# Order of the routing steps in a turn of the dilated attention: picks one head later, gate steps dealt one to a head, the gates' turn at the ninth head

## The reference, cut to what matters

```python
t = t + _L3_attn_ref(_ln_t(t), ...)        # 16 heads of 8; segments of 256, 512, ... tokens, dilations 1, 2, ...
# of _L3_ffn_ref(_ln_t(t), ...), the routing:
gate_logits = x @ gate_weight.T            # 16 experts
top_vals, top_idx = jax.lax.top_k(gate_logits, 2)
routing_w = jax.nn.softmax(top_vals, axis=-1)
```

## Time and profile before

| | us |
|---|---|
| median of 3 runs | 3617.76 (3611.89 to 3627.61) |
| the profiled execution | 3635.59 |
| its span, first to last instruction | 3633.8 |
| PE busy | 2827.6 (78%) |
| DVE busy | 2208.3 (61%) |
| ACT busy | 1549.9 (43%) |
| POOL busy | 1040.7 (29%) |
| mean granted TensorE clock | 0.884 |

### The profile page before, as it was taken

The page is one execution under the profiler, slowest core; times in us unless marked ns, Lnnn a source line. Parts: engine busy times, 40 slices in busy tenths (PEclk is TensorE's granted clock), DMA queues, the critical chain, the costliest instruction groups (busy, mean ns, idle before and its releaser), DMA issues. The chain is left out here.

```text
span 3633.8 us, 65093 instructions
## 1 busy us (share of the span) xinstructions
PE 2827.6 (78%) x20886; PEld 1553.7 (43%) x20887; DVE 2208.3 (61%) x4232; ACT 1549.9 (43%) x3274; POOL 1040.7 (29%) x1360
## 2 busy tenths in 40 slices
PE   6777849999999999996599119558888888619998
PEld 3334503433343334332598117435555555403336
DVE  5774547777777777772222116547777777526771
ACT  1113516666666666664355003424444444404440
POOL 0002300122222222223233752214565565620000
PEclk8998959999999999999799559868998888859995
DMA  2002442132213232310322113332333223021123
GB/s 76 0 0 102 184 84 39 37 52 45 51 39 53 42 54 39 53 25 11 103 61 60 41 41 111 103 55 54 60 64 63 61 58 62 24 90 50 51 57 117
DMA packets 209243, 215.62 MB, mean 59 GB/s; under 512 B 33456, under 2 KB 185201, under 8 KB 209009
## 3 DMA queue, kind: packets, MB, share of 16 engines
q1 hardware_dynamic: 187008, 178.05, 21.8%
q0 software_dynamic: 14336, 25.72, 2.7%
q10 hardware_dynamic: 7680, 8.93, 0.7%
HBM read 129.26 MB, written 81.90 MB: 58 GB/s over the span
## 5 line engine op out<-in xcount | busy, mean ns | idle before, releaser
L1539 ACT ACTIVATE attn_exps<-attn_sbank 128x392 f32<-128x392 f32 x1600 | 704.6, 503 | 499.3 <-PE attn_sbank L1456 493.6
L1581 DVE TENSOR_REDUCE attn_mx<-attn_rot 128x1 f32<-128x784 f32 x768 | 722.3, 967 | 191.8 <-PE attn_rot L1469 188.0
L1469 PE MATMUL attn_rot<-attn_k,attn_q 96*128 96x392 bf16 x1536 | 401.6, 344 | 97.1 <-DVE attn_mx L1581 64.6
L2223 ACT ACTIVATE dil_exps<-dil_sbank 128x512 f32<-128x512 f32 x512 | 289.2, 597 | 407.3 <-PE dil_sbank L2121 338.1
L1456 PE MATMUL attn_sbank<-attn_q,attn_k 99*128 99x392 bf16 x1536 | 450.1, 333 | 12.3 <-ACT attn_exps L1539 11.1
L1496 PE MATMUL attn_acc<-attn_exps,attn_v 128*32 128x392 f32 x3584 | 348.4, 500 | 0.0
L2274 DVE TENSOR_REDUCE dil_mx<-dil_rot 128x4 f32<-128x1024 f32 x256 | 307.6, 1219 | 55.4 <-PE dil_rot L2131 53.2
L2131 PE MATMUL dil_rot<-dil_k,dil_q 96*128 96x256 bf16 x1024 | 174.2, 299 | 120.3 <-DVE dil_mx L2274 83.2
L1456 PEld LDWEIGHTS attn_sbank<-attn_q,attn_k 99*128 99x128 bf16 x1536 | 148.8, 98 | 270.1 <-ACT attn_exps L1539 133.9
L2661 PE MATMUL silu_ph<-silu_route_w,silu_xT 128*128 x424 | 237.7, 645 | 22.6 <-issue 11.2
L1469 PEld LDWEIGHTS attn_rot<-attn_k,attn_q 96*128 96x128 bf16 x1536 | 117.5, 99 | 303.5 <-DVE attn_mx L1581 201.6
(11 more groups left out here) (370 smaller groups left out, 4863.5 us busy)
## 6 DMA issues: line engine op xcount, KB each, us to landing
attn_q<-q_pieces SPq DMA_DIRECT2D x192, 98.0 KB
attn_k<-k_pieces SPq DMA_DIRECT2D x192, 98.0 KB
silu_x<-silu_rows SPq DMA_DIRECT2D x212, 64.0 KB
dil_q<-dil_q_pieces SPq DMA_DIRECT2D x192, 66.0 KB
dil_k<-dil_k_pieces SPq DMA_DIRECT2D x192, 66.0 KB
q_pieces<-qkv_piece SPq DMA_DIRECT2D x16, 588.0 KB, 3.1
k_pieces<-qkv_piece SPq DMA_DIRECT2D x16, 588.0 KB, 3.2
v_rows<-qkv_v SPq DMA_DIRECT2D x16, 476.0 KB, 3.8
```

Of the source, the lines that this page charges most:

```text
L1469: ins = nc.tensor.matmul(rot[b][:, hf, 0:HS], q[nxt.side][g][0:QROWS, j, c * P:(c + 1) * P], k_[nxt.side][g][0:QROWS, j, cols], start=True ...
L1539: nc.scalar.activation(e_[:, n % NP, :], sbank[(n + t.side) % 3][:, 0:HS], ACT.Exp, scale=A_DIM ** -0.5).then_inc(s_ex, 1)
L1581: nc.vector.tensor_reduce(into, rot[b][:, :, 0:HS], AX.XY, ALU.max).then_inc(s_free, 1)
L2223: nc.scalar.activation(e_[:, k % NP, :], sbank[k % 3][:], ACT.Exp, scale=D_DIM ** -0.5).then_inc(s_ex, 1)
```

## The change

It moves steps in the list and nothing else; no operation is added, dropped or resized.

```diff
             out += [("ranks", lag), ("soft", lag)] + [("place", n, lag) for n in range(5)]
         if h >= 2:
             out.append(("scatter", h - 2, lag))
-        if h == 2:
-            out += [("place", n, lag) for n in range(5, 11)]
-        return out + {4: [("gate", lag)], 5: [("store", lag)]}.get(h, [])
+        if 2 <= h <= 7:
+            out.append(("place", h + 3, lag))
+        if h == 8:
+            out += [("gate", lag), ("store", lag)]
+        return out
...
-                out += [("pick", n) for n in range(16) if 11 + (n + 2) // 4 == h] + [("root",)] * (h == 12)
+                out += [("pick", n) for n in range(16) if 12 + n // 4 == h] + [("root",)] * (h == 12)
```

## The result

The changed kernel takes **3592.60 us** (median of 6 runs, 3585.77 to 3601.91), the kernel before 3615.66 us beside it (6 runs, 3605.21 to 3627.61): a ratio of 0.9933, 95% interval 0.9909 to 0.9957. That is 23 us faster. The forecast was 3575, 43 us faster.

The account below looks back on a forecast made before the run. A full turn was taken as a chain alternating between PE and DVE, neither full. Terms -4.6 + 0.1 + 1.3 + 0.3 = -2.9 us, times 13 -38, last turns -6: -43 from 3617.76 to 3575 us, range 3560 to 3605.

Parts of the forecast that it names:

- Stretch A: From `turn` 1's copy to the sixth head's maximum: gates leaving h=2 to 4 save 4.6 us a turn at full clock.
- B: From the sixth to the tenth head's maximum: +1.3 us for the gates' transposes, +0.1 for small operations.
- h=8: New place of the gates' transposes, ahead of the weighing: +1.3 us a turn, bounds 0.84 and 2.2.
- Picks: Late in the turn, POOL's scaling of the rows holds pick 13 (L937): +0.3 us a turn, bounds -0.3 and +0.3.
- C: From the rows' copy to the next turn's first maximum, where moved picks stand: +0.3 us a turn.
- the 0.5 us that the prediction named as a sign of being wrong: Late in the turn: held picks adding up to more than 0.5 us a turn would refute the forecast.
- SP's queue: `store` at h=8 delays SP's loads 4 to 5 us; about 5 us slack, nothing charged; slower rival 3639 us, chance 0.05.
- which one?: Gain between `turn` 1's copy and the sixth maximum: 4.6 us at the upper clock, 2.9 if the dip stays; took 4.6.
- where the prediction wanted to see 1.00: Sign expected from `turn` 1's copy to the sixth maximum: granted clock 1.00, the 2.4 GHz level.
- the dip stays (or moves along the stretch): Rival, chance 0.22: low clock remains behind 1.29 us of idle PE; gain 2.9 instead of 4.6, -22 in all, 3596 us.
- The tails: Turns 15 and 16: PE's waits ahead of `compact` leave, partly returning ahead of `add`; 0 to -10 us, -6 taken.

Follow-up runs that it names:

- e1_picks_only: The kernel before with only the picks' places moved, gate steps as before: 3621.23 us, ratio 0.9996.
- e4_norm_late: The changed kernel with POOL's scaling of the rows tied to pick 15 instead of pick 9: 3573.31 us, ratio 0.9871.
- e3_fill: The changed kernel with PE's four transposes of `turn` 1 done five times over, same values, same place: 3583.08 us, ratio 0.9896.
- e6_fill14: The changed kernel with POOL's scaling tied to pick 15 and PE's fill at h=14 written five times: 3611.25 us, ratio 0.9976.
- e7_fill_both: The changed kernel with POOL's scaling at pick 15, and both the h=14 fill and `turn` 1's transposes written five times: 3606.70 us, ratio 0.9949.
- e11_gate13_oldpicks: The changed kernel with the gates' transposes and store at h=13 instead of h=8, picks where they were before: 3612.21 us, ratio 0.9978.

## Why the forecast came out as it did

**The mechanism was right for turns whose clock stays up in A and B.** *Stretch A*: forecast 4.6 us less at full clock; 5.92 us instead of 10.54, in every turn whose clock stays up. *h=8*: forecast +1.3 for the transposes and +0.1 for the small operations; B rose from 8.79 to 10.11, by 1.32, and in the shorter turn the transposes wait 0.49 us for `place` 10, as forecast. *Picks*: +0.3 with bounds of -0.3 and +0.3; C rose by 0.15, in the changed kernel and in `e1_picks_only` alike. The pick that the scaling holds is L947 for 2.2 us, not L937 for 1.3; what it costs is small for the reason given, since PE's second fill is next in line: `e4_norm_late` takes the hold away and gets 0.45 us. By their length the two holds (0.7 and 2.2 us) pass the 0.5 us that the prediction named as a sign of being wrong; by what they cost a turn they don't. *SP's queue*: in the turns that I read it appears nowhere as a releaser of scores. `turn` 0's DMAs start 3.8 us later than before against the sixth maximum (14.3 behind it, 10.5 before), about the delay that was counted. The some 5 us for their landing rested on no row, since the trace gives no landing for them. Such a turn comes to 44.8 us, forecast 45.

**The term that was mis-sized is the clock's.** The text asked "which one?", 4.6 or 2.9, and took 4.6 for all turns because the 2.02 us of idle PE would go. The changed kernel does both, turn by turn: seven of twelve turns have the low clock in the stretch, where the prediction wanted to see 1.00. In six of them it stands behind the 1.29 us that stay. Such a turn costs 2.6 us more than the other kind, 1.3 in A (the rival said 1.7) and 1.2 to 1.5 in B, where the rival had 0.3. Thirteen turns so gave 21.4 us in place of 38. The rival "the dip stays (or moves along the stretch)" described most turns. That its -22 stands near the 23 us of the medians is in part luck: it took the dip for every turn and priced it too low. The Trainium skill (TensorE: Matmul & The Clock Gate, What's actually happening) says that activity releases the throttle. The places that were filled agree: the clock is up there in `e3_fill` and at 1.00 in `e6_fill14` (2704 to 2711). It doesn't follow that the turn gets shorter, since other places of `e6_fill14` lost the clock.

**The tails came out as forecast, as far as can be told.** The two profiles give 13.2 us by the last two intervals against 6 (and past its end of 10), but 5.8 of them are the late `dil_rec` of before; against `e1_picks_only` they are 6.2. PE in the changed kernel, turns 15 and 16:

```profile
3093.65 0.83 PE L1063 MATMUL dil_rot<-dil_ident,dil_r_gate 112*16 112x112 f32 x7 [1.18 <-DVE dil_r_gate L1058]
...
3119.24 1.08 PE L2169 MATMUL dil_rot<-dil_o,dil_den_c 128*32 128x128 f32 x32 [0.16 <-ACT dil_o L2241]
...
3127.26 1.46 PE L1063 MATMUL dil_rot<-dil_ident,dil_r_gate 112*16 112x112 f32 x7 [1.06 <-DVE dil_r_gate L1058]
```

The waits of 2.62 and 4.86 us became 1.18 and 1.06, both behind `compact` now. So part of them came back ahead of `add`, as forecast: 2.2 us. The transposes are shorter in turn 15 (0.83 us, before 1.38) and not in turn 16 (1.46, before 1.47).

**What stays open.** Why a turn falls into one kind or the other isn't shown. It isn't the idle time next to the place alone: the 1.29 us stand in both kinds. In several kernels the turns lock to one length with the low clock at the same places of each turn (`e4_norm_late` 44.4, `e7_fill_both` and `e11_gate13_oldpicks` 47.8), so the position seems to depend on the whole turn before; that is argued, not shown. Open too is what held DVE in turn 16 of before, and whether its other runs have it: before has only one profile. The 14.3 us ahead of the turns have no cause in the change: in seven experiments that leave everything ahead of it as it was, the first `dil_rec` stands anywhere from 2442.8 to 2454.1.

## What to carry to other kernels

Price a moved step by an iteration that already lacks it, if the trace has one: turn 1 gave the new stretch to the hundredth of a us. Look for the place where the engine waits for a third engine whatever it does (PE for ACT at h=14 here) before one where it only seems to have time; that was worth 26 to 32 us more. Where the granted clock changes within a turn, give each level its own forecast and expect a mixture, and don't judge an edit by its own stretch, since a low clock that is driven from one place may come back in a dearer one. When an engine gets faster, look at what it then meets: here DVE, once PE no longer kept it waiting, ran into POOL's scaling and lost 2.8 us a turn. Hold a pair of profiles against the medians before you explain their difference.

## What the runs showed that I had not expected

The same instructions in the same order take 44.8 or 47.4 us a turn within one execution, by the granted clock alone.

Repeating work to keep PE busy saved some 10 us against the changed kernel in one place (the intervals overlap) and cost 38 against `e4_norm_late` in another, there together with POOL's new hold on DVE.

L947, which reads and writes SBUF alone, started at 2755.41 inside POOL's indirect DMA (2755.07 to 2756.04) and ended 0.14 us behind the tensor operation that came next on POOL. The indirect DMA by itself doesn't hold such operations: L928 took 0.27 us inside another one (2748.48, POOL from 2748.37 to 2749.31), and in `e4_norm_late` L947 took 0.41 us from the same point of the same DMA (2710.22, POOL from 2709.88), with only a short operation behind it. So in the changed kernel it was the scaling that held it, from 0.4 us or more ahead of the scaling's recorded start; why so early isn't shown, and POOL's spans are rough. Others that meet a POOL operation end the same distance behind it: L928 of `e11_gate13_oldpicks` at 2777.81, with L2094 there ending at 2777.68. The Trainium skill (SBUF — State Buffer, SBUF: two separate sides) calls the port pair an exclusive lock that goes to whoever starts first. That one blocks the other agrees with these rows; who comes first doesn't, by the recorded starts of L947 and the scaling.
